# Two local-attention layers of a fused block: the softmax division moved from the probabilities to the mixed values, through a DRAM copy of the reciprocals, with new instruction orders

## The chip, the cores and the metric

The kernel runs on one core of one Trainium2 chip. A core has TensorE (PE; its weight loads are listed apart as PEld), VectorE (DVE), ScalarE (ACT), GpSimd (POOL) and SyncE (SP), which here only issues DMAs. The metric is device time in microseconds (us) of one execution; lower is better. Each engine works through its own list of instructions in order, and waits on semaphores where it needs another engine's result.

## The reference

32 sequences of 256 rows by 128 columns in float32 pass through four residual blocks: full attention with 16 heads and a feed-forward layer; causal attention with rotary positions; and two layers, each of local attention and a gated feed-forward. Only the local attention is touched. For each of its 8 heads of 64 columns:

```python
sim  = einsum('bhwid,bhwjd->bhwij', bq, bk)     # l2-normed, rotary q and k; window of 64 plus the one before
sim  = where(mask, -finfo.max, sim)
attn = softmax(sim, axis=-1)
out  = einsum('bhwij,bhwjd->bhwid', attn, bv)   # heads joined, then x = x + out @ wo
```

## The kernel before

The work of one sequence is cut into six streams, written as digits in the orders: 0 is the first attention with its feed-forward (ATTN0), 1 the causal attention (ATTN1), 2 and 3 the two local attentions (LOCAL0, LOCAL1), 4 and 5 the feed-forward layers behind them (FEED0, FEED1). A stream is a list of units ("qkv2", "scores2", "turn_p", ...), and a unit has a share of work on some of the engines. Different sequences are in work at one time, one stream's behind the other's.

Each engine's order is written out by hand as strings of digits: FIRST fills the pipeline, TURNS is repeated ROUNDS times, and LAST drains it. One repetition (a round) takes one unit list of each stream, so one sequence's worth of work. FIRST and LAST together hold 954 units of each engine's list, a round 159, so they hold six sequences' worth and the 26 rounds the other 26. The eight PSUM banks are handed out by strings of digits too. STEADY_FILLERS and END_FILLERS name units ahead of which PE runs matmuls without use (L1031), which keep it busy where it would wait; 488 are issued in all, 11 of them in each round.

The local attention's softmax: "scores2" fills two banks with queries 0 to 127 and then four with queries 128 to 255 (L1206, L1212); DVE takes negated maxima (L980); ACT takes the exponent with a running sum (L792) into P0, which lies in rawP, and P1, both in SBUF; "norm2", in two halves of four heads, makes reciprocals of the sums on DVE (L987) and multiplies P0 and P1 in place (L990); "turn_p" transposes one head's probabilities on PE (L1224 to L1226), and waits at heads 0 and 4 for the half of norm2; ACT copies them out (L797); "mix2" multiplies with the values (L1239), four heads a bank, and DVE copies the bank to o2T, which lies in rawB (L917); "project2" follows (L1247), and DVE adds the residual into YB (L941).

SP serves three kinds of unit: "residual" loads the next sequence (L583), "shift_rows" moves rows of YB to feed_h (L589, L590), "finish" stores an output (L595). Before each it waits for its own condition, in order.

Of the kernel before, what the change touches and what calls it, by code (L numbers as in the profile page):

```python
# [9 lines left out]
P = 128  # L10
# [17 lines left out]
def shape_constants():  # L28
# [29 lines left out]
    def table(c, s):  # L58
# [15 lines left out]
ROUNDS = 26  # L74
# [4 lines left out]
        "0000000000000000000000000000000000000000000000111100000010000111010011000000100000011100001001100111"  # L79
        "1000101111002222111112221001022202222220111100112222222220000100202111000002222220000102202221101102"  # L80
        "1121000110110022111112222210144442220222221111010140442002222224132220000333003332023330003333300222"
        "2221110000210202220211011200110333333333130113113002222333333111110013333312222223011110311444402222"
        "2444002222222242255551353335000050020250001233"
    ),
    "scalar": (
        "0000000000000000000000000000000000000000001110000000010010000111100000000000000011111100001111111000"
        "0000011110022111111222221001002222222211112222222220000000200220000111111002222220000122222111111000"
        "0000111102220021111112222214444122200111122222004442222222322200000003330033322000033300333332222221"
        "1111100001222221111000000110333333333301111332220022211111133333300133333122222211110044444222224442"
        "2222222225555333333000000055500220000111123345"  # L90
    ),
    "vector": (
        "0000000000000000000000000000000000010001000000000110000100000000001111101100000010000000001111001111"
        "0111111111000012222221120012220000222222200001111122220111222220000020220000000022222011110110222220"
        "2111111111114414222222110000001222222002222211111100222244440000401333333222223000002012330003333333"
        "3222222000000022222001111211433331111114333331113113140000222222003111003333333333222232222222511111"
        "0012254444522004001033333315555222220000002250"
    ),
    "gpsimd": (
        "0000000000000000000000000000000000101111000000000000000000000000000000001111111111101111111111111112"  # L100
        "2222112221222222222222000000000000000000000000000000001111111111111111111111111442222222222222222222"
        "2222221112122222220444444222222200000000000000000000000000000003333333333303333333331111111111111111"
        "1111111114412222222222222222222222222211221222222222422205554444400000000000000000000000000555553333"
        "3333333333333333333333000000001111111122222222"
    ),
    "sync": (
        "0000000000000000000000000000000000000000000000000000000000000000000000000000000000000000000004000000"
        "0000000000000000000000000004444444450000000000000000000000000000000000000000001111111111111111111111"
        "1111111111111111111111111111111111111111111111111111111111111111111111111111112222222222222222222222"
        "2222222222222222222222222222222222222222222222222222222222222222222222222222222222222233333333333333"  # L110
        "3333333333333333333333333333333344444445555555"
# [4 lines left out]
        "3333002222200001210102222101201123333311003033333331330113113002222111113333330031133303444422232222"  # L116
        "22221111301401244022222220422132300003305555505550250001233"
    ),
    "scalar": (
        "3003332222200001112222211113333311300000003333333330111133222002333333221111110013333314444222222111"  # L120
        "12222200424422222222233300000003555553300555220000111123345"
    ),
    "vector": (
        "3003333333333222222000000111102222201102433331111114333331113110000313224222200333331100133333222232"
        "22222255111110012244442200540050122222333333555510000020520"
    ),
    "gpsimd": (
        "3333333333311133311111111111111442222222222222222251112122444444222222222222550000000000000000000000"
        "00000000333333333333333333333333330555555001111111122222222"
    ),  # L130
    "sync": (
        "4550000000000000000000000000000000001111111111111111111111111111122222222222222222222222222222222222"
        "22222333333333333333333333333333333333333333344444445555555"
# [4 lines left out]
        "3100222223330000120333333102222011201121133333333300101103113020211111220333330311333332220222222221"  # L138
        "3111031144440444222222222200413555553333330000555002201133315222222122222112333332113333333311313113"
        "1132222111112223333331333333444412224311114412222224222222222315555531332555233311153331222222112222"  # L140
        "2112333332113333333333111311322224444222333333333332223434422222243322222222333335555533325552253333"
        "3322222222222333333333233233333333333344443444433333333335555555533333333333333333533333333333335555"
        "55555115"
    ),
    "scalar": (
        "3100222223330000133333312222211111133333333300000000111133222002221111113333300313331332222222222211"
        "1100444444422222222223335555533333300000005550022111113331222222122222113333311333333331133111133222"
        "2221111113333332223333314444412221111444222222222222222333555555333555221111133313331222222112222211"
        "3333311333333333311113322222244444333333222333332224443332222222222222333555555233323335552233333322"
        "2222222223333333333333333333333444444443333333333335555555553333333333333333333333333333555555555011"  # L150
        "12233455"
    ),
    "vector": (
        "3002333333333300000222220011112222202033111133111133333111300001144132222220031110023333333333222222"
        "2222435511111100222244454000045103333155553332222220000225333333333322222222223324111133111111411333"
        "3311131131322222223333341133333132222222222554444111112222545113333222223355155225333323333333222221"
        "1112222211233334111111433333111314332222222333332233333222222223444445522225533333335555222222333333"
        "3333522332222233222223333332333333344433333344444555333333353333333333555533333333333533333333333355"
        "55555555"
    ),  # L160
    "gpsimd": (
        "3353333333333111113311111111111112222222222222222221112244222222222244444422550000000000000000000000"
        "0000000033333333333333333333333335555553333333331111111111133311531133111111111114422222222222222222"
        "2222222222211222444444122222222255333333333333333333333335335555533333353311111111111311333113331111"
        "1111442222222222222222222222222222444444222222222222553333333333333333333333333555555333333333333333"
        "4444444455533333333333333333333333333333333313333333555555555555555522222222222222222222333333333333"
        "33333333"
    ),
    "sync": (
        "5455555555544444444555555555444444445444444445555555555555555550000000000000000000000005555555500000"  # L170
        "0111111111111111111111111111111111111111111111111111111111111111111111111112222222222222222222222222"
        "2222222222222222222222222222222222222222222222222222222222222222222222222222222222222222222222222222"
        "2222222333333333333333333333333333333333333333333333333333333333333333333333333333333333333333333333"
        "3333333333333333333333333333333333333333333333333333333333333333333333333333333333333333333333333333"
        "34444444"
    ),
}
FIRST_BANKS = (
    "6704365530407614536573225450135701574201526701547040270216460734252673765021624735015647135023047562"
    "1732072413462505231403062564073240156752135461327050327650411705347357012455265347156207561454071536"  # L180
    "1720450635426537210265410653207615260357132065426312504617325041643013675236103752405167265263762451"
    "6475304052174571054603125034761520163241034257504136273506325470231542106437126034741526307134251674"
    "1067453123056102736045372067513245703642707351203476103642753167524375046310120571324507316254741530"
    "27161235647131067574014356204"
)
# [157 lines left out]
def fused_block(nc, x, wqkv0, w1_0, b1_0, w2_0, b2_0, wqkv1, wo1, wqkv2, q_scale, k_scale, wo2,  # L343
# [7 lines left out]
    with ExitStack() as ctx:  # L351
# [651 lines left out]
        def _(pe):  # L1003
# [13 lines left out]
            def unit(u):  # L1017
# [198 lines left out]
                elif u.kind == "turn_p":  # L1216
# [5 lines left out]
                    for sem, count in newest(free(u)):  # L1222
                        pe.wait_ge(sem, count)
# [77 lines left out]
```

## Time and profile before

| | us |
|---|---|
| median of 3 runs | 2964.49 (2964.08 to 2968.03) |
| the profiled execution's own time | 2968.08 |
| its span, first to last instruction | 2966.4 |
| PE busy | 2714.0 (91%) |
| DVE busy | 2337.2 (79%) |
| ACT busy | 2126.4 (72%) |
| POOL busy | 1606.6 (54%) |

Busy time is a union of an engine's instructions; matmuls overlap one another, so the mean of one times the count is more than the busy time. The share is over the whole span, with its filling and draining.

### The profile page before, as it was taken

Reading aid. Unit: us, or ns where it says so; the run is one execution under the profiler, and the core shown is the slowest. Engines: PE = TensorE matmul, PEld = TensorE weight load, DVE = VectorE, ACT = ScalarE, POOL = GpSimd, SP = SyncE. Lnnn points to the kernel's source line nnn. Section 1 sums busy time; section 2 is a strip of 40 time slices with the busy share of each in tenths; the row PEclk is TensorE's granted clock in tenths of the full one; section 3 lists DMA queues with packets and bytes.
Section 4 is the critical chain, followed back from the end, with each engine's and each line's share of the span. In section 5 each row is a group of like instructions: output and inputs, shape, how many; then the busy total and the mean of one; then the engine's idle time right before and its main releaser. Section 6 shows DMA issues by size and latency. Waiting matters only on the chain.

```text
span 2966.4 us, 69962 instructions
## 1 busy us (share of the span) xinstructions
PE 2714.0 (91%) x24680; PEld 1949.3 (66%) x24680; DVE 2337.2 (79%) x5888; ACT 2126.4 (72%) x5956; POOL 1606.6 (54%) x1747
## 2 busy tenths in 40 slices
PE   5778999999999999999999999999999999999887
PEld 3445666666666676666667666666766666676665
DVE  3467778888888888888888888888888888887764
ACT  2356687777778777877877777787777778777663
POOL 1035455565555556555655655565565556556653
PEclk8889999999999999999999999999999999999999
DMA  2000000000000000000000000000000000000000
GB/s 80 3 3 4 5 4 7 5 6 7 7 7 4 7 5 6 7 7 7 5 6 5 6 7 7 7 5 6 5 7 6 7 7 5 6 7 5 5 3 8
DMA packets 41990, 22.72 MB, mean 8 GB/s; under 512 B 21130, under 2 KB 40884, under 8 KB 41652
## 3 DMA queue, kind: packets, MB, share of 16 engines
q1 hardware_dynamic: 41652, 18.24, 2.2%
q8 instruction: 209, 3.42, 0.5%
q14 instruction: 129, 1.06, 0.1%
HBM read 9.86 MB, written 4.19 MB: 5 GB/s over the span
## 4 chain that ended last, share of the span: by engine, by line
PE 53%; ACT 25%; DVE 16%; issue 3%; POOL 2%; DMA 0%; SPq 0%; DVEq 0%; POOLq 0%; ACTq 0%
PE bank L1175 8%; DVE negmax L900 7%; PE bank L1075 6%; ACT P L792 5%; ACT probs L760 5%; PE bank L1247 4%; PE bank L1186 4%; PE bank L1140 3%; PE bank L1255 3%; ACT rawP L792 3%; PE bank L1239 3%; PE bank L1031 3%; PE bank L1212 3%; PE bank L1096 2%; PE bank L1206 2%
## 5 line engine op out<-in xcount | busy, mean ns | idle before, releaser
L760 ACT ACTIVATE probs<-bank 128x512 f32<-128x512 f32 (+1 forms) x1024 | 478.1, 568 | 206.2 <-PE bank L1119 205.4
L900 DVE TENSOR_REDUCE negmax<-bank 128x2 f32<-128x512 f32 (+1 forms) x896 | 555.1, 683 | 54.4 <-PE bank L1096 40.5
L1175 PE MATMUL bank<-wqkv_sb,hS 128*128 128x512 f32 x768 | 399.8, 623 | 23.2 <-ACT rawA L797 12.4
L692 POOL TENSOR_TENSOR rn<-ss_kept,minus_half 128x16 f32<-128x16 f32 x128 | 372.7, 2912 | 64.8 <-DVE ss_kept L960 64.8
L637 POOL TENSOR_TENSOR veps<-moments,eps_tile 128x2 f32<-128x2 f32 x192 | 38.9, 203 | 641.9 <-DVE moments L852 640.8
L659 POOL TENSOR_SCALAR_AFFINE_SELECT probs<-probs 128x256 f32<-128x256 f32 x512 | 200.2, 413 | 234.8 <-ACT probs L760 234.5
L1140 PE MATMUL bank<-probs,V 128*16 128x256 f32 (+1 forms) x4096 | 246.7, 359 | 25.1 <-POOL probs L659 18.4
L680 POOL TENSOR_TENSOR rawA<-rawA,rope_sb 128x512 f32<-128x512 f32 x128 | 186.3, 1456 | 90.4 <-ACT rawA L779 90.3
L980 DVE TENSOR_REDUCE negmax<-bank 128x2 f32<-128x384 f32 (+1 forms) x384 | 207.1, 595 | 35.0 <-PE bank L1212 34.8
L680 POOL TENSOR_TENSOR rawB<-rawB,rope_sb 128x512 f32<-128x512 f32 x128 | 177.7, 1388 | 85.5 <-ACT rawB L779 85.3
L792 ACT ACTIVATE P<-bank,negmax 128x192 f32<-128x192 f32 x512 | 208.4, 453 | 5.2 <-DVE negmax L980 3.4
L914 DVE COPY rawC<-bank 128x256 f32<-128x256 f32 x256 | 105.7, 414 | 130.1 <-PE bank L1140 129.9
L1175 PEld LDWEIGHTS bank<-wqkv_sb,hS 128*128 128x128 f32 x768 | 125.4, 192 | 106.8 <-issue 78.3
L1255 PE MATMUL bank<-feed_hT,w_sb 128*128 128x256 f32 (+1 forms) x768 | 189.0, 390 | 3.6 <-ACT feed_hT L721 1.3
L1140 PEld LDWEIGHTS bank<-probs,V 128*16 128x16 f32 x4096 | 96.1, 96 | 146.2 <-issue 67.7
L751 ACT ACTIVATE qT<-bank 128x512 fp32r<-128x512 f32 x256 | 153.8, 667 | 45.7 <-PE bank L1075 45.5
L946 DVE TENSOR_REDUCE ss<-P 128x8 f32<-128x512 f32 x256 | 173.1, 676 | 16.4 <-ACT P L776 12.6
L792 ACT ACTIVATE rawP<-bank,negmax 128x128 f32<-128x128 f32 x512 | 180.2, 377 | 6.3 <-DVE negmax L980 5.7
L1031 PE MATMUL bank<-ident_r 128*128 128x512 f32 x488 | 162.0, 449 | 23.1 <-ACT P L792 8.7
L687 POOL TENSOR_TENSOR rawA<-rawA,rawQ 128x512 f32<-128x512 f32 x128 | 163.7, 1279 | 33.6 <-DVE probs L868 33.6
L751 ACT ACTIVATE kT<-bank 128x512 fp32r<-128x512 f32 (+1 forms) x256 | 145.7, 646 | 45.0 <-PE bank L1186 43.6
L687 POOL TENSOR_TENSOR rawB<-rawB,rawP 128x512 f32<-128x512 f32 x128 | 175.5, 1371 | 0.0
(140 smaller groups left out, 7293.7 us busy)
## 6 DMA issues: line engine op xcount, KB each, us to landing
xin<-x SPq DMA_DIRECT2D x32, 128.0 KB, 2.1
out<-xout SPq DMA_DIRECT2D x32, 128.0 KB, 1.8
feed_h<-YB SPq DMA_DIRECT2D x64, 63.5 KB
wqkv_sb<-wqkv SPq DMA_DIRECT2D x1, 1536.0 KB
feed_h<-YB SPq DMA_DIRECT2D x64, 0.2 KB
rawQ<-c_masks SPq DMA_DIRECT2D x1, 832.0 KB
w_sb<-w SPq DMA_DIRECT2D x1, 682.0 KB
w_sb<-w SPq DMA_DIRECT2D x2, 256.0 KB, 2.9
```

The costliest lines, as they stand in the source:

```text
L680: nc.gpsimd.tensor_tensor(raw, raw, tab, ALU.mult).then_inc(sig("cos_part", u), 1)
L687: nc.gpsimd.tensor_tensor((q2, k2)[m][:, l, t, :], (q2, k2)[m][:, l, t, :], sines[m][:, l, t, :], ALU.add)\
L692: nc.gpsimd.tensor_tensor(rn[:, l, t].rearrange("p m h -> p (m h)"), ss_kept[:, l, t].rearrange("p m h -> p (m h)"), minus_half[:], ALU.po ...
L751: nc.scalar.activation(dst[:, 2 * u.part:2 * u.part + 2, :].rearrange("p g q -> p (g q)"), tile(u)[:], ACT.Copy).then_inc(has_emptied(u), 1)
L760: nc.scalar.activation(dst, src, ACT.Exp, scale=SCALE0 if k == ATTN0 else SCALE1)\
L792: last = nc.scalar.activation(dst, src, ACT.Exp, bias=negmax[:, k, t, hd:hd + 1], accum_out=expsum[:, l, t, hd:hd + 1])
L900: nc.vector.reduce_max(negmax[:, k, t, head:head + 4 * many - 3:4], tile(u, e)[:, :].rearrange("p (h k) -> p h k", h=many), AX.X, negate=T ...
L980: nc.vector.reduce_max(dst, src, AX.X, negate=True).then_inc(sig("max_done", u), 1)
L1031: mm(tile(u, spare)[:].rearrange("p (a k) -> p a k", a=4), ident_r[:], ident_r[:].unsqueeze(1).broadcast_to([P, 4, P]), start=True, stop=T ...
L1140: last = mm(tile(u)[32 * n:32 * n + 16, q0:SEQ], V[:, k, t, 4 * g + n, :], part, start=t == 0, stop=t == 1)
L1175: mm(tile(u)[:], hS[:, l, t * P:(t + 1) * P], wqkv2_sb[:, l, m * INNER:(m + 1) * INNER], start=True, stop=True).then_inc(has_filled(u), 1)
L1255: last = mm(tile(u)[0:n, half * SEQ:(half + 1) * SEQ], w1_2_sb[:, l, half * HID + at:half * HID + at + n], hT[k], start=True, stop=True)
```

## The change

"norm2" goes. A unit "spread2" of each local layer takes its place: DVE makes all reciprocals in one instruction of 128x16; PE transposes them, two instructions of 128x8, into rows of heads; ACT copies 8x256 to SBUF (recip_T); SP writes these 8 KB to DRAM (recip_kept), waits until they have landed, and issues two DMAs which each read one 4 KB line back to 64 partitions, 256 KB each, into recip_rows, which is the place of kT2. "turn_p" waits for the exponents alone. DVE's copy of the mixed values becomes a multiplication with recip_rows, and the first of the two waits for the DMAs.

```diff
-    units += [Unit("norm2", half, rec_done=1, p_ready=1) for half in range(2)]
+    units += [Unit("spread2", bank=1, rec_done=1, rows_out=16, rows_spread=2 * 16)]
...
+        recip_rows = kT2
+        recip_T = sb("recip_T", [HEADS, 2, SEQ])
+        recip_kept = nc.dram_tensor("recip_kept", (2, 2, PAIRS * SEQ), f32, kind="Internal").ap()
...
+                elif u.kind == "spread2":     # SP
+                    for sem, count in newest(taken(u)):
+                        sp.wait_ge(sem, count)
+                    sp.dma_start(recip_kept[l].rearrange("e (c q) -> (e c) q", c=PAIRS), recip_T[:, l, :])\
+                        .then_inc(sig("rows_out", u), 16)
+                    sp.wait_ge(sig("rows_out", u), so_far("rows_out", u) + 16)
+                    for e in range(2):
+                        sp.dma_start(recip_rows[HD * e:HD * e + HD, l, :, :].rearrange("p c q -> p (c q)"),
+                                     recip_kept[l, e].partition_broadcast(HD)).then_inc(sig("rows_spread", u), 16)
...
+                elif u.kind == "spread2":     # ACT
+                    nc.scalar.activation(recip_T[:, l, :], tile(u)[0:HEADS, 0:SEQ], ACT.Copy).then_inc(has_emptied(u), 1)
...
                 elif u.kind == "mix2":        # DVE
+                    if u.part == 0:
+                        dve.wait_ge(sig("rows_spread", u), so_far("rows_spread", u))
-                    nc.vector.tensor_copy(o2T[:, l, 2 * u.part:2 * u.part + 2, :].rearrange("p c q -> p (c q)"), tile(u)[:])\
+                    nc.vector.tensor_tensor(o2T[:, l, own, :].rearrange("p c q -> p (c q)"), tile(u)[:],
+                                            recip_rows[:, l, own, :].rearrange("p c q -> p (c q)"), ALU.mult)\
...
-                elif u.kind == "norm2":       # DVE
-                    nc.vector.reciprocal(recip[:, k, :, own], expsum[:, l, :, own]).then_inc(sig("rec_done", u), 1)
-                    for t, part, n in ((0, P0[:, l, own], P), (1, P1[:, l, own, WINDOW:SEQ], SEQ - WINDOW)):
-                        last = nc.vector.tensor_tensor(part, part, recip[:, k, t, own].unsqueeze(2).broadcast_to([P, 4, n]), ALU.mult)
+                elif u.kind == "spread2":     # DVE
+                    nc.vector.reciprocal(recip[:, k, :, 0:HEADS].rearrange("p t (e c) -> p t c e", e=2),
+                                         expsum[:, l, :, :].rearrange("p t (c e) -> p t c e", e=2)).then_inc(sig("rec_done", u), 1)
...
+                elif u.kind == "spread2":     # PE
+                    pe.wait_ge(sig("rec_done", u), so_far("rec_done", u) + 1)
+                    for t in range(TT):
+                        last = turn(tile(u)[0:HEADS, t * P:(t + 1) * P], recip[:, k, t, 0:HEADS], ident)
```

All orders and bank strings are new. There are 27 rounds of 157 units, and FIRST and LAST hold 785 units, five sequences' worth. Where the old strings take long runs of one stream, the new ones change streams almost at every digit:

```diff
 TURNS "tensor"
-        "3333002222200001210102222101201123333311003033333331330113113002222111113333330031133303444422232222"
+        "2223410120244400224152235054435030030033202333005103255030233232121000012022221103350331123011023333"
...
-STEADY_FILLERS = {(ATTN0, "scores", 1): (3, 0), (ATTN0, "maxes", 1): (3, 1), (ATTN1, "scores", 0): (3, 0), (LOCAL0, "qkv2", 0): (2, 0)}
+STEADY_FILLERS = {(LOCAL1, "mix2", 1): (4, 0), (LOCAL1, "spread2", 0): (3, 0), (LOCAL0, "scores2", 1): (3, 0)}
```

A new round has 10 fillers and the whole kernel 452. In a new round the units that PE's list has between the two parts of "scores2", and from there to "spread2", are these. LOCAL0: "down0", three fillers, the second part, a "qkv2" of LOCAL1, "down2", a "turn", a "qkv2" of LOCAL1, "spread2". LOCAL1: a "turn" of ATTN1, "project1", the second part, a "mix" and a "scores" of ATTN0, "shift", three fillers, "spread2". DVE's list has between "spread2" and the first "mix2" of LOCAL0: two "qkv2" and two "scale2" of LOCAL1, "down2", two "qkv" of ATTN0; of LOCAL1: an "apply" of ATTN1, two "qkv2" and "norms2" of LOCAL0, two "mix" of ATTN0, two "qkv" of ATTN1. ACT's list has just ahead of the first "scores2" two "up0" for LOCAL0, and a "scores" of ATTN0 and a "turn" for LOCAL1. PE's list has between "spread2" and the first "mix2" four "turn_p" and seven to nine units of other streams.

## Rows read from the trace of the kernel before

**Rows 1.** Busy time by stretch: PE, PEld, DVE, ACT, POOL, clock, DMA share, GB/s.

```profile
0.00:200.00 200.00, 133.99 (x1016) 87.41 (x1016) 92.56 (x260) 72.18 (x158) 44.69 (x70) 0.84 0.10 32
...
1000.00:1500.00 500.00, 476.57 (x4476) 343.37 (x4476) 418.26 (x1058) 379.71 (x1059) 287.39 (x316) 1.00 0.02 6
...
1507.46:1593.81 86.35, 82.25 (x768) 59.34 (x767) 72.42 (x184) 66.10 (x188) 50.19 (x55) 1.00 0.02 6
```

**Rows 2.** Chain of work that ended last, 1500 to 1700 us: start, us, what.

```profile
1507.46 1.10 DVE rawP L990
...
1587.63 1.28 ACT L792
1588.92 2.90 ACT rawP L792 x16
...
1593.81 1.10 DVE rawP L990
1594.90 1.94 DVE P L990
...
1603.64 0.89 PE bank L1031 x3
...
1604.98 0.89 PE bank L1031 x3
...
1680.11 1.11 DVE rawP L990
```

**Rows 3.** Groups by line and shape, whole span: count, busy us, mean ns, idle before.

```profile
L990 DVE TENSOR_TENSOR P<-P,recip 128x768 f32<-128x768 f32 x128 | 150.3, 1174 | 0.0
L990 DVE TENSOR_TENSOR rawP<-rawP,recip 128x512 f32<-128x512 f32 x128 | 100.5, 785 | 4.4
L987 DVE RECIPROCAL recip<-expsum 128x8 f32<-128x8 f32 x128 | 24.8, 194 | 15.5 <-ACT P L792 15.3
L923 DVE RECIPROCAL recip<-bank 128x16 f32<-128x16 f32 x128 | 32.1, 251 | 49.7 <-PE bank L1147 49.7
L917 DVE COPY rawB<-bank 128x512 f32<-128x512 f32 x128 | 86.9, 680 | 15.5 <-PE bank L1239 15.4
L946 DVE TENSOR_REDUCE ss<-P 128x8 f32<-128x512 f32 x256 | 173.1, 676 | 16.4 <-ACT P L776 12.6
L951 DVE TENSOR_TENSOR rawQ<-bank,rope_sb 128x256 f32<-128x256 f32 x128 | 52.7, 411 | 0.0
L969 DVE TENSOR_TENSOR rawB<-rawB,rn 128x512 f32<-128x512 f32 x128 | 100.9, 788 | 2.0 <-POOL rawB L687 2.0
L724 ACT ACTIVATE probs<-bank 128x256 f32<-128x256 f32 x128 | 55.2, 431 | 128.7 <-PE bank L1052 128.6
L1168 PE MATMUL bank<-w_sb,rawC 128*128 128x128 f32 x512 | 64.6, 280 | 1.1 <-issue 1.0
```

**Rows 4.** DMA issues, whole span: count, KB each, median us to landing.

```profile
xin<-x SPq DMA_DIRECT2D x32, 128.0 KB, 2.1
out<-xout SPq DMA_DIRECT2D x32, 128.0 KB, 1.8
...
w_sb<-w SPq DMA_DIRECT2D x2, 256.0 KB, 2.9
```

**Rows 5.** The same chain, 2780 to 2967 us.

```profile
2945.62 0.56 SPq L589
2946.23 5.37 DMA feed_h<-YB
```

**Rows 6.** SP's queue: waits in all, times, longest us.

```profile
SPq L588 <- DVE YB L941: 1578.6, 64, 44.2
```

**Rows 7.** The chain again, 1500 to 1700 us: single units of PE and ACT.

```profile
1539.56 0.71 PE bank L1153 x4
1540.27 0.90 PE bank L1206 x8
1541.17 0.66 PE bank L1212 x7
1541.85 0.57 DVE negmax L980
1542.44 3.33 ACT P L792 x16
...
1546.44 2.07 ACT probs L760 x4
...
1565.29 0.51 PE bank L1119 x8
...
1568.62 0.99 PE bank L1140 x16
...
1575.22 1.34 PE bank L1263 x12
...
1578.36 0.37 PE bank L1052 x2
...
1581.57 0.86 PE bank L1175 x2
...
1585.09 1.46 ACT rawC L766 x4
```

More of the change, by code:

```diff
@@ L156 @@
[L156 to L159, printed above, removed]
+        "1331222222225111105244405222540001053532232213351025102030223313233353333112212323322123331323111131"
+        "1214314131422342312211321333233332223252211222121152444223545152222513233332523123523231323313333231"
@@ L168 @@
+        "3432333332533343423333322434333343342333254532333333332333335533335355333525335533235332232333555353"
+        "325335333"
     ),
     "sync": (
[L170 to L173, printed above, removed]
@@ L176 @@
+        "33555555555"
     ),
@@ L196 @@
+    "432337435162741562156236036476504610"
 )
-STEADY_FILLERS = {(ATTN0, "scores", 1): (3, 0), (ATTN0, "maxes", 1): (3, 1), (ATTN1, "scores", 0): (3, 0), (LOCAL0, "qkv2", 0): (2, 0)}
+STEADY_FILLERS = {(LOCAL1, "mix2", 1): (4, 0), (LOCAL1, "spread2", 0): (3, 0), (LOCAL0, "scores2", 1): (3, 0)}
 END_FILLERS = {
-    (0, ATTN0): {("turn_q", 0): 5, ("mix", 0): 7, ("mix", 1): 7, ("mix", 2): 7, ("mix", 3): 7, ("turn", 0): 8},
-    (1, ATTN0): {("turn_q", 0): 5, ("mix", 0): 7, ("mix", 1): 3, ("mix", 2): 7, ("turn", 0): 8},
-    (31, LOCAL1): {("qkv2", 2): 9, ("turn_p", 0): 10},
-    (31, FEED1): {("turn", 0): 28},
+    (0, ATTN0): {("maxes", 1): 6, ("maxes", 2): 4, ("maxes", 3): 7, ("mix", 0): 7, ("mix", 2): 4},
+    (1, ATTN0): {("maxes", 1): 6, ("maxes", 3): 6, ("mix", 0): 7},
+    (0, LOCAL0): {("shift", 0): 5, ("turn_q2", 0): 6},
+    (1, LOCAL0): {("shift", 0): 5},
+    (2, ATTN1): {("maxes", 0): 6},
+    (30, LOCAL0): {("shift", 0): 6},
+    (31, ATTN1): {("maxes", 1): 4},
+    (31, LOCAL0): {("scores2", 1): 7},
+    (30, LOCAL1): {("spread2", 0): 11},
+    (30, FEED1): {("turn", 0): 8},
+    (31, LOCAL1): {("turn_q2", 0): 6},
+    (31, FEED1): {("turn", 0): 27, ("down2", 0): 5},
@@ L1216, in unit @@
                 elif u.kind == "turn_p":
+                    needs = [free(u)]
                     if u.part % 4 == 0:
-                        made = earlier(u, "norm2", u.part // 4)
-                        pe.wait_ge(sig("p_ready", made), so_far("p_ready", made) + 1)
+                        first, second = (taken(earlier(u, "scores2", n)) for n in range(2))
+                        needs += [first, second[0:2]] if u.part == 0 else [second[2:4]]
                     hd, bank = u.part, tile(u)
-                    for sem, count in newest(free(u)):
+                    for sem, count in newest(*needs):
                         pe.wait_ge(sem, count)
```

140 lines of the change are left out of this document (65 added, 75 removed).

## The prediction

> **What bounds the kernel now.** I read the busy time by stretch first [rows 1]. In the middle PE is busy 476.6 of 500 us, DVE 418.3, ACT 379.7, at a granted clock of 1.00; at the start PE has 134.0 of 200 at 0.84. So there are two parts, a steady one and two ends. Then the chain [rows 2]: the same multiplication of rawP (L990) stands at 1507.46 and at 1680.11, two rounds later, so a round is 86.33 us. In one round [rows 1] PE is busy 82.25 us and idle 4.1, and DVE is busy 72.4.
>
> 26 rounds take 2244.6 us, which leaves 721.8 us of the span of 2966.4 for the ends, with six sequences' worth of units. Six rounds would be 518.0; the ends therefore cost 203.8 us beyond their work.
>
> The chain says what holds the round. It passes from engine to engine: ACT's table load and exponents (1.28, 2.90, 1.62), then 1.10 + 1.94 us of L990 on DVE, later PE, with six fillers in it (0.89 + 0.89) [rows 2]. The reader is to see that the removed multiplication stands in a place where the work behind it waits: 3.04 us in each round.
>
> **What goes.** L990 is 150.3 + 100.5 us in all [rows 3], 7.84 us a sequence on DVE. The four reciprocals of 128x8 (194 ns) become two of 128x16, nearest the 251 ns of L923 [rows 3]: 0.27 us less. On DVE's list that is 8.1 us of 72.4. Only what is on the chain counts for the end: 3.04 us a round. The rest of L990 (4.8 us a round) is in the chain nowhere, and I count it as nothing; if the chain came to pass there, the round could shrink on, and then PE's own work stands in the way, which is the first rival.
>
> **What comes in its place.** The mixed values' multiplication reads PSUM and SBUF, 128x512. Its bounds are the copy that it replaces, 680 ns (L917), and a multiplication of that shape with both inputs in SBUF, 788 ns (L969) [rows 3]; four times a sequence 0 to 0.4 us, and I take 0, since with PSUM as one input it is nearer the copy.
>
> PE gets four transposes a sequence. A "turn" of two has 0.37 us [rows 7], so at most 0.74 us and, with only 8 columns to load, not under 0.2; I take 0.44. It loses one filler of 0.30 [rows 2]. Net 0.1.
>
> ACT gets two copies of 8x256. The nearest is 128x256, 431 ns (L724) [rows 3]. ACT's stretch of the chain holds one of them: 0.43 us. Nothing or both would be 0 or 0.86.
>
> The sum for a round: 86.33 - 3.04 + 0.1 + 0.43 = 83.8 us.
>
> **The trip through DRAM.** After the last exponent: reciprocal 0.25, transposes 0.4, copy 0.43, write, read. No row shows a write of 8 KB or two reads of 256 KB. For the write the nearest are the store of an output, 1.8 us, and the load of a sequence, 2.1 [rows 4]; the farthest is feed_h, whose issue and landing take 0.56 + 5.37 us [rows 5]. For the reads the nearest is a 256 KB load, 2.9 us [rows 4], for both together if they overlap and 5.8 if not. I take 2.1 + 3.5, because the sizes are those of the first rows, so 6.7 us in all. With 0.2 for the transposes, 1.8 and 2.9 it is 5.6, with 0.74, 5.93 and 5.8 it is 13.1.
>
> The Trainium skill (DMA: Bandwidth & Descriptors, Anatomy of one DMA) speaks against such a trip: each DMA has a fixed cost of about 2.0 us, mostly the receipt of the write, heaviest to HBM, and bytes come on top at 436 GB/s. As an estimate from that page the write and the two reads overlapped would be 5.2 us in place of 5.6. The trace's 1.8 to 2.9 us for 128 to 256 KB agrees; no run here shows the small write. Neither changes the round.
>
> What hides it: PE has four turn_p and seven to nine other units before "mix2", and DVE has two qkv2 (2 x (0.68 + 0.41 + 0.41) = 3.0 us) and, in LOCAL0, two scale2 (1.6) before it multiplies [rows 3]. So DVE, held at the head of its list, may wait 6.7 - 4.6 and 6.7 - 3.0, at most 5.8 us a round, and at the far bound 18.6. Behind it wait ATTN0's maxima in LOCAL0 and LOCAL1's next qkv2, and PE for their banks. DVE is then busy 64.4 of 83.8 us: idle 19.4. I take the wait as covered by that. SP's own list is held through write and issue, some 3 us twice a round; behind it stand shift_rows and the loads, and SP now waits up to 44.2 us for them [rows 6], so this is nothing.
>
> **The ends.** FIRST and LAST go from 954 to 785 units. The 203.8 us may shrink with the units, to 167.7, or stay, if they are one sequence's latency; nothing shows which, and I take the middle, 186.
>
> Span: 32 x 83.8 + 186 = 2868. The profiled execution's own time was 1.7 us over its span, and the median 3.6 below that own time, so 1.9 less: **2866 us**.
>
> **Rivals.**
>
> *Deeper* (chance 0.17). Without the stop at norm2, the six fillers in the chain fall out of it too: 83.8 - 1.8 = 82.0, and the ends go with the units: 32 x 82.0 + 168 = 2792, reported 2790. For it: the fillers stand where PE waited for DVE. Against it: this is under PE's 82.25 busy us of today. But a busy PE here overlaps its matmuls: single units run at 0.86 us for two of 512 columns [rows 7]. The Trainium skill (Perfetto Trace Analysis, Identifying the Most-Contended Engine) says the same: matmul busy share is no measure of how near PE is to its peak, weight loads are. The trace has those at 59.3 of 86.35 us [rows 1], which by that rule leaves room below 82.
>
> *Elsewhere* (0.17). A path beside L990, of nearly its length, takes over, for DVE's freed time is spread and PE and ACT have as much to do as before. The round stays 86.3: with ends of 186 a reported 2947, with 204 no change, 2965. For it: PE is idle in many short gaps, not one. I give two thirds to the first, since fewer units are in the ends.
>
> *Slower* (0.18). In PE's list "spread2" stands soon after "scores2", and waits for the last exponent and the reciprocal, with everything of PE's behind it. From the end of the first "scores2", ACT's side is [rows 7, 2] maximum 0.57, load 1.28, exponents 2.90 + 3.33, reciprocal 0.25: 8.3 us in LOCAL0, and 7.05 without a load in LOCAL1. PE's side in LOCAL0: down0 2.0 (64.6 us over 32, L1168 [rows 3]), fillers 0.9, second part 0.90 + 0.66, qkv2 0.86, down2 1.34, turn 0.37, qkv2 0.86: 7.9. In LOCAL1: turn 0.37, project1 0.71, second part 1.56, mix 0.99, scores 0.51, shift 0.37, fillers 0.9: 5.4. PE waits 0.4 + 1.65 = 2.05 us a round, if ACT is at once free; in its list two up0 (1.46) and an ATTN0 scores (2.07) stand just ahead, so up to 5.6. The forecast takes these waits to fall into the 4.1 us a round that PE is idle today. If that idle time stays beside them, all of it lengthens the round, and it decides from 3.3 us: (2972 - 186) / 32 = 87.1, against 83.8. Half-way from there to the top, 4.4: 32 x 88.2 + 186 = 3008, reported 3006. Against it: the second part needs PE at once, but the first part's exponents are half done by then.
>
> **How the numbers follow.** The forecast has 0.48. A measurement of this kernel can tell about 0.2%, 6 us. Faster: 0.48 + 0.17 + 0.11 = 0.76; same 0.06; slower 0.18. The range goes from 2775, half a us a round (16 us) under the deeper case, to 2970, the no-change end of the third rival; the slower case and a little of the deeper one are left out. The forecast's own range, with 0.1 to 0.8 us each way on ACT's and PE's terms and 167.7 to 203.8 for the ends, is 2830 to 2900.
>
> **What would show it.** Right: L990 gone, the distance between repeats of one line near 83.8 us, DVE busy near 64 of it, ACT near 67, PE idle under 4 us, and the chain passing from the exponents into turn_p. The multiplication near 0.7 us. The DMA's landing before DVE comes to mix2, so that its list of waits has little for recip_rows. Wrong: a wait of PE for the reciprocal at spread2 of over 3 us a round (slower); the chain through SP's DMAs and DVE's multiplication (the trip is not hidden, which a landing over 10 us would do); a round of 86 us with DVE idle (elsewhere); a granted clock under 1.00 in the middle, since gaps would then cost PE's speed as well.

## The result and the profile after

The changed kernel takes 3013.31 us (median of 4 runs, 3012.73 to 3014.28) against 2964.47 (2964.08 to 2968.03) for the kernel before: a ratio of 1.0162, 95% interval 1.0145 to 1.0180. It is slower, by 49 us or 1.6%: clear of the noise, though less than 2%. Forecast were 2866 us and a range from 2775 to 2970.

The first view is busy time by stretch, columns as in [rows 1]: 500 us of the middle, then three neighbouring rounds of the changed kernel. A round is taken here from one last addition of an output on POOL to the next.

```profile
1000.00:1500.00 500.00, 470.59 (x4433) 339.87 (x4435) 380.20 (x981) 381.54 (x1072) 275.45 (x309) 0.99 0.07 19
1527.62:1615.67 88.05, 83.09 (x772) 60.03 (x771) 67.00 (x173) 66.68 (x189) 48.52 (x55) 0.98 0.07 18
1615.67:1703.75 88.08, 83.16 (x773) 60.42 (x772) 66.95 (x173) 66.66 (x189) 48.47 (x55) 0.98 0.07 18
1703.75:1790.40 86.65, 81.71 (x772) 59.47 (x771) 66.67 (x173) 66.67 (x189) 48.48 (x55) 1.00 0.07 18
```

Against the round in [rows 1], DVE's busy time fell from 72.4 to 67.0 us, and ACT has 66.7 as forecast; still no round is under 86.6. There are two kinds of round: 16 of 24 take 88.0 to 88.1 us at a clock of 0.98, every third about 86.65 at 1.00. This pattern runs through the whole steady part. Read in windows of 0.1 us, 24 rounds from the first have a mean of 87.59 us; those of before have 86.39.

So the 46.2 us between the spans (3012.6 and 2966.4) divide as follows. 26 rounds take 2277.1 us where before's would take 26 x 86.39 = 2246.1: 31.0. Of these, 26 x (87.59 - 86.65) = 24.4 come from the rounds with the lower clock, the other 7 from 86.65 against 86.39. What lies around these 26 rounds, six sequences' worth of work in both kernels, grew from 720.3 to 735.5: 15.2.

The chain of work that ended last, in one stretch of such a round (start, us, what):

```profile
1579.66 1.79 PE bank L1265 x16
1581.67 1.13 PE bank L1100 x13
1583.51 1.58 ACT probs L768 x3
1586.26 1.84 PE bank L1149 x16
1588.10 3.42 PE bank L1273 x12
...
1675.57 4.05 PE bank L1273 x12
```

L990 is gone from the chain [rows 2]. In its place PE's own matmuls are the chain: by engine, PE holds 67% of the span in the page's chain and DVE 17%, where before it was 53% and 16%, with 25% on ACT. And the same twelve matmuls of "up2" (L1273) that take 2.79 us in the round ahead of these (at 1500.52, a short one) take 3.42 and 4.05 here. Why is told by windows of 1 us, same columns; the first five from the round that starts at 1527.62, the last four from the one that starts at 1703.75:

```profile
1583.00:1584.00 1.00, 0.48 (x16) 0.27 (x12) 1.00 (x5) 0.49 (x1) 0.22 (x1) 1.00 0.02 0
1584.00:1585.00 1.00, 0.00 (x0) 0.00 (x0) 1.00 (x3) 1.00 (x4) 1.00 (x1) 1.00 0.06 12
1586.00:1587.00 1.00, 1.00 (x16) 0.32 (x12) 0.87 (x3) 0.88 (x1) 1.00 (x2) 0.50 0.08 18
1588.00:1589.00 1.00, 1.00 (x6) 0.84 (x3) 1.00 (x4) 0.00 (x0) 1.00 (x1) 0.50 0.00 0
1590.00:1591.00 1.00, 1.00 (x7) 0.76 (x6) 0.82 (x2) 0.61 (x2) 0.92 (x2) 1.00 0.00 0
...
1760.00:1761.00 1.00, 0.00 (x0) 0.00 (x0) 1.00 (x3) 1.00 (x3) 1.00 (x1) 1.00 0.04 10
1761.00:1762.00 1.00, 0.69 (x21) 0.72 (x24) 1.00 (x3) 0.98 (x3) 1.00 (x1) 1.00 0.08 18
1762.00:1763.00 1.00, 1.00 (x28) 0.45 (x20) 0.93 (x3) 1.00 (x1) 1.00 (x2) 1.00 0.08 17
1764.00:1765.00 1.00, 1.00 (x6) 0.88 (x5) 1.00 (x3) 0.47 (x1) 1.00 (x2) 1.00 0.01 1
```

PE stops at the same place in both rounds. In the first the granted clock then falls to 0.50, the lower of its two levels (1.2 GHz), from 1586 to beyond 1589; in the other it stays at 1.00. The clock behind the stop costs 1.4 us (88.05 and 86.65); what the stop costs without it is left to run 3. PE's timeline names the place (start, us, what, idle before it):

```profile
1582.63 0.56 PE L1105 MATMUL bank<-kT,qT 32*128 32x128 f32 x16
1583.03 0.45 PE L1128 MATMUL bank<-qT,kT 32*128 32x256 f32 x8
1585.18 0.51 PE L1105 MATMUL bank<-kT,qT 32*128 32x256 f32 x8 [1.71 <-ACT probs L768]
```

L1105 is ATTN1's "maxes", L1128 ATTN0's "scores". The new order of PE has ATTN1's first "maxes" (banks 2, 6, 1, 4), ATTN0's last "scores" (0, 7, 5, 3) and ATTN1's second "maxes" (2, 5, 7, 6) right behind one another: twelve uses of eight banks, so PE waits for ACT's exponents (L768) to give a bank back. Before, an "up2" and a "mix" of one bank each stood between the two "maxes" (0347, then 5 and 6, then 0423), and neither kernel has fillers there. The old order has twelve uses in a row at another place (ATTN0's first "maxes" 4017, ATTN1's first "scores" 2546, ATTN0's second "maxes" 2310), and there three fillers stand ahead of the second unit and three ahead of the third.

The change's own parts, by groups (line, shapes, count, busy us, mean ns, idle before) and DMA issues:

```profile
L931 DVE TENSOR_TENSOR rawB<-bank,kT 128x512 f32<-128x512 f32 x128 | 87.7, 686 | 68.4 <-PE bank L1257 48.6 <-DMA kT<-recip_kept 19.7
L1243 PE MATMUL bank<-ident_r,recip 128*8 128x128 f32 x128 | 24.7, 275 | 16.2 <-DVE recip L999 16.2
L809 ACT ACTIVATE recip_T<-bank 8x256 f32<-8x256 f32 x64 | 23.0, 359 | 2.4 <-PE bank L1243 2.4
L999 DVE RECIPROCAL recip<-expsum 128x16 f32<-128x16 f32 x64 | 16.3, 254 | 59.6 <-ACT P L800 58.1
...
kT<-recip_kept SPq DMA_DIRECT2D x128, 256.0 KB, 3.8
...
out<-xout SPq DMA_DIRECT2D x32, 128.0 KB, 3.6
```

The multiplication takes 686 ns (the copy had 680 [rows 3]), the reciprocal 254, ACT's copy 359, the two reads 3.8 us. DVE idles for the DMA in 7 of its 128 multiplications, 19.7 us in all, and the list of waits has none of these in five rounds of the middle: the trip is hidden.

DVE's busy time fell by 5.4 us a round and not by the 8.1 that were to go. The largest part of the rest is a multiplication that the change does not touch and that takes longer in the new orders; first before, then after:

```profile
L969 DVE TENSOR_TENSOR rawA<-rawA,rn 128x512 f32<-128x512 f32 x128 | 93.1, 728 | 10.2 <-POOL rawA L687 10.1
```
```profile
L984 DVE TENSOR_TENSOR rawA<-rawA,rn 128x512 f32<-128x512 f32 x128 | 133.0, 1039 | 9.0 <-POOL rawA L695 6.6 <-issue 0.3
```

Without the DMAs of the reciprocals (run 4) it still takes 1037 ns, so it is not they; what it is stays open.

### The profile page after: what moved, and what is told of

It reads as the page before. It is cut to its first block, busy times and chain, and to the rows that moved or that the text cites. A ratio compares the mean times of both kernels' runs of the same rounds, so it can differ in the third digit from the quotient of the medians.

```text
span 3012.6 us, 70452 instructions
## 1 busy us (share of the span) xinstructions
PE 2732.9 (91%) x24772; PEld 1966.2 (65%) x24772; DVE 2154.7 (72%) x5568; ACT 2145.9 (71%) x6020; POOL 1561.6 (52%) x1747
## 4 chain that ended last, share of the span: by engine, by line
PE 67%; DVE 17%; ACT 8%; issue 4%; POOL 1%; DMA 1%; DVEq 0%; SPq 0%; POOLq 0%; ACTq 0%
DVE negmax L911 8%; PE bank L1184 8%; PE bank L1273 6%; PE bank L1084 6%; PE bank L1149 5%; PE bank L1257 4%; PE bank L1195 4%; PE bank L1265 4%; ACT P L800 4%; PE bank L1067 3%; DVE negmax L995 3%; PE bank L1221 3%; PE bank L1105 2%; PE bank L1215 2%; ACT probs L768 2%
## 5 line engine op out<-in xcount | busy, mean ns | idle before, releaser
L768 ACT ACTIVATE probs<-bank 128x512 f32<-128x512 f32 (+1 forms) x1024 | 472.5, 548 | 204.9 <-PE bank L1128 204.2
L645 POOL TENSOR_TENSOR veps<-moments,eps_tile 128x2 f32<-128x2 f32 x192 | 49.9, 260 | 609.8 <-DVE moments L863 609.0
L1149 PE MATMUL bank<-probs,V 128*16 128x256 f32 (+1 forms) x4096 | 262.3, 376 | 10.7 <-ACT probs L768 5.5
L1273 PE MATMUL bank<-feed_hT,w_sb 128*128 128x256 f32 (+1 forms) x768 | 206.7, 416 | 6.4 <-DVE up2T L1005 3.4
L688 POOL TENSOR_TENSOR rawB<-rawB,rope_sb 128x512 f32<-128x512 f32 x128 | 165.3, 1292 | 70.7 <-ACT rawB L787 70.7
L759 ACT ACTIVATE qT<-bank 128x512 fp32r<-128x512 f32 x256 | 140.0, 597 | 85.7 <-PE bank L1084 85.6
L1105 PE MATMUL bank<-kT,qT 32*128 32x256 f32 (+1 forms) x2048 | 117.8, 313 | 87.4 <-ACT probs L768 57.6
L1273 PEld LDWEIGHTS bank<-feed_hT,w_sb 128*128 128x128 f32 (+1 forms) x768 | 145.7, 198 | 71.7 <-issue 25.4
L695 POOL TENSOR_TENSOR rawB<-rawB,rawP 128x512 f32<-128x512 f32 x128 | 162.8, 1272 | 54.4 <-DVE probs L879 54.4
L813 ACT ACTIVATE up2T<-bank,b_sb 128x256 f32<-128x256 f32 (+1 forms) x192 | 90.6, 473 | 130.8 <-PE bank L1273 128.0
L1105 PEld LDWEIGHTS bank<-kT,qT 32*128 32x128 f32 x2048 | 82.4, 187 | 141.6 <-DVE negmax L911 57.4
```

The costliest lines, as they stand in the source:

```text
L688: nc.gpsimd.tensor_tensor(raw, raw, tab, ALU.mult).then_inc(sig("cos_part", u), 1)
L768: nc.scalar.activation(dst, src, ACT.Exp, scale=SCALE0 if k == ATTN0 else SCALE1)\
L1105: last = mm(tile(u, e)[:, i * keys:(i + 1) * keys], qT[rows, k, first + i, t * P:(t + 1) * P], kT[rows, k, first + i, 0:keys], start=not w ...
L1149: last = mm(tile(u)[32 * n:32 * n + 16, q0:SEQ], V[:, k, t, 4 * g + n, :], part, start=t == 0, stop=t == 1)
L1273: last = mm(tile(u)[0:n, half * SEQ:(half + 1) * SEQ], w1_2_sb[:, l, half * HID + at:half * HID + at + n], hT[k], start=True, stop=True)
```

## The experiments

Two theories stood after this profile. **Clock** (Theory A in the expectations): the stop at ATTN1's second "maxes" and the clock behind it are the loss. **Change's own**: the reciprocal's way is, by PE's wait at "spread2" (Theory B) or by DVE's wait for the DMAs (Theory C). Beside them stood the forecast's own question: what is L990 worth in the chain?

| run | us | ratio to before, 95% | clock | mean round |
|---|---|---|---|---|
| before | 2964.47 | | 0.982 | 86.39 |
| after | 3013.31 | 1.0145 to 1.0180 | 0.968 | 87.59 |
| 1 old orders, new arithmetic | 3173.01 | 1.0670 to 1.0710 | 0.953 | 93.12 |
| 2 new orders, old arithmetic | 3190.20 | 1.0716 to 1.0790 | 0.939 | 93.53 |
| 3 after, two fillers at "maxes" | 2986.52 | 1.0052 to 1.0086 | 0.980 | 86.66 |
| 4 after without the trip | 3009.46 | 1.0129 to 1.0163 | 0.970 | 87.47 |
| 5 after without the division | 3024.98 | 1.0180 to 1.0211 | 0.968 | 88.14 |
| 6 before without the division | 2957.57 | 0.9952 to 0.9978 | 0.983 | 85.90 |
| 7 run 1 without the trip | 2988.35 | 1.0059 to 1.0089 | 0.981 | 86.78 |
| 9 run 3, seven fillers fewer | 2981.87 | 1.0039 to 1.0069 | 0.983 | 86.67 |
| 10 after, one "up2" moved | 2990.33 | 1.0065 to 1.0095 | 0.980 | 86.82 |
| 11 run 10, seven fillers fewer | 2985.62 | 1.0047 to 1.0077 | 0.979 | 86.83 |
| 12 before, six fillers fewer | 2983.94 | 1.0039 to 1.0072 | 0.971 | 86.97 |
| 13 run 6, six fillers fewer | 2958.55 | 0.9964 to 0.9986 | 0.978 | 86.24 |

Clock is the mean granted clock of the profiled execution; the mean round is over 24 rounds, by the outputs' additions. The intervals are those of the ratio to runs of the kernel before on the same chip (2966.73 us beside runs 10 to 13). Runs 4 to 7 and 13 leave out the division or part of its way, so they compute something else. The profiled execution of run 6 is the fastest of its five (2950.13 us; the others take 2957.4 to 2957.6). There is no run 8.

**Runs 1 and 2: each half alone.**

```diff
 # 1: on before; orders, banks and fillers as they were, but for spread2's bank, its place in ACT's list, and SP's list
-    units += [Unit("norm2", half, rec_done=1, p_ready=1) for half in range(2)]
+    units += [Unit("recip2", rec_done=1), Unit("spread2", bank=1, rows_out=16, rows_spread=2 * 16)]
 # 2: on after; one norm2 (both halves) where spread2 stood
-    units += [Unit("spread2", bank=1, rec_done=1, rows_out=16, rows_spread=2 * 16)]
+    units += [Unit("norm2", rec_done=2, p_ready=2)]
```

> The old orders, banks and fillers, with the new arithmetic put into them: the reciprocals at the place of the first norm2, transposes, copy and DMAs at that of the second. Theory A (the loss lies in the new orders: a stop of PE with no fillers in it, after which the granted clock falls in most rounds): the arithmetic by itself costs nothing or helps, 2900 to 2965 us. Theory B (PE's wait for the reciprocal at spread2 is the loss, some 2.5 us a round): this one waits as well, 2990 to 3040 us. Theory C (DVE held by the DMAs at mix2): in these orders DVE comes to mix2 sooner after the reciprocal, over 3040 us.

> The new orders, with norm2 (both halves) at the place of spread2, no transposes, copies or DMAs of reciprocals. Theory A: the stop and the falling clock stay, and DVE has its 8 us a round back, 3010 to 3080 us. Theory B: PE has no spread2 to wait at, but turn_p waits for the multiplications, so between 2940 and 3010 us. Theory C: 2940 us or less.

Both are some 7% slower, rounds of 93 us. Run 1 lies in the range of Theory C; Theory A had the arithmetic cost nothing there, and missed. Run 2 lies above all the ranges. In run 1 the trip has come into the chain; its largest wait of DVE over the span, and two lines of its chain:

```profile
DVE rawB L985 <- DMA kT<-recip_kept: 215.8, 59, 9.1
...
1508.89 1.28 DMA recip_kept<-recip_T
1510.79 4.79 DMA kT<-recip_kept
```

In run 2 PE stops at "turn_p" for a bank that DVE empties late: its list has both halves of norm2, 5.9 us, ahead of that:

```profile
1515.58 0.33 PE L1220 MATMUL bank<-ident_r,rawP 128*128 128x128 f32 x1 [3.57 <-DVE rawQ L948]
```

So the new orders hide the trip, where the old ones with spread2 in this place do not, and the old arithmetic does not fit the new orders. Whether another place in the old orders would hide it was not tried. Both runs also lose by the clock: in 24 rounds it falls to 0.50 in 34 stretches of run 1 and in 51 of run 2. The rounds at a clock of 1.00 take 90.1 to 90.3 us in run 1 and 89.9 in run 2.

**Run 3: fillers at the stop.**

```diff
-... (LOCAL0, "scores2", 1): (3, 0)}
+... (LOCAL0, "scores2", 1): (3, 0), (ATTN1, "maxes", 1): (2, 0)}
```

> The changed kernel with two more fillers in each round, ahead of ATTN1's second maxes, in the bank that comes free first, where PE stops for 1.7 us and the clock falls behind it. Theory A: the clock stays at 1.00, 1.0 to 1.4 us a round are won, 2970 to 2985 us. Theory B and C: two fillers more and nothing won, 3013 to 3030 us.

Two matmuls without use in each round save 27 us. The clock is 1.00 all through the middle, and every round takes 86.6 to 87.0 us: the long rounds are gone, and no short one got shorter. That is the clock theory, and its size (24.4 us in the steady part). The stop without the falling clock cost nothing: filled, the round is as long as the short rounds that have it. The time is 1.5 us over the range of Theory A.

**Runs 4 and 5: the change's own costs, in the new orders.**

```diff
 # 4: no SP part; mix2 multiplies by a constant tile in SBUF
-    recip_rows[:, l, own, :].rearrange("p c q -> p (c q)"), ALU.mult)
+    wqkv2_sb[:, l, 0:512], ALU.mult)
 # 5: spread2 empty on all engines; mix2 copied; its three fillers ahead of turn_p
-                elif u.kind == "spread2":   # PE, ACT, DVE, SP
```

> The changed kernel without the DMAs of the reciprocals: mix2 multiplies by a tile of weights and waits for no DMA, so the division is left out; reciprocals, transposes, copies and fillers stay. DVE's list of waits in the changed kernel shows next to nothing for recip_rows, so the trip is hidden in these orders and this is within 0.5% of the changed kernel, 3000 to 3020 us. If the trip is on the path, 2960 us or less.

> The changed kernel with no division at all: no reciprocals, transposes, copies, DMAs and multiplications of them (mix2 is copied out as before); the softmax's division is left out. Its three fillers of spread2 stand before turn_p. Theory A: turn_p waits for the same exponents, the stop at maxes stays, 2985 to 3010 us. Theory B: some 2.5 us a round are won, 2920 to 2945 us. Theory C: 2940 us or less.

Without the trip 4 us are saved, as expected. Without reciprocals, transposes, copies, trip and multiplication the kernel is no faster (run 5 lies above all three ranges) and has the long rounds more often, 20 of 24. Run 5 is not a clean removal: "spread2" and its fillers had covered PE's wait ahead of LOCAL0's first "qkv2", and now PE stops there too:

```profile
1570.55 1.12 PE L1159 MATMUL bank<-wqkv_sb,hS 128*128 128x512 f32 x2 [1.32 <-ACT hS L724]
```

But the rounds in which the clock holds have only the stops themselves and no slow matmuls behind them: they take 86.65 us after, 86.57 in run 4 and 86.86 in run 5. Taking out the change's own arithmetic wins nothing back there either.

**Runs 6 and 7: the same parts in the old orders.**

```diff
 # 6: norm2 empty; turn_p waits for the exponents only
-    units += [Unit("norm2", half, rec_done=1, p_ready=1) for half in range(2)]
+    units += [Unit("pause2", half) for half in range(2)]
 # 7: run 1 without the SP part; mix2 multiplies by a constant tile
```

> The kernel before, orders, banks and fillers unchanged, with norm2 left out and nothing in its place: the softmax's division is left out, turn_p waits for the exponents alone. It is the most that any replacement of norm2 can give in these orders. If the step of 3.04 us a round on the chain was right, 2964 falls by some 95 us, to 2860 to 2880. If the freed time of DVE is worth little, because PE's list and its banks hold the round, 2930 to 2966.

> The old orders with the new arithmetic, without its DMAs: reciprocals, transposes and copies are made, mix2 multiplies by a tile of weights in place of the spread reciprocals and waits for no DMA, so the division is left out. If the DMAs' landing is what makes the old orders with the new arithmetic 207 us slower than before, this is within 40 us of the kernel without the division, under 3000 us. If spread2 on PE and ACT (its bank, its wait) is, it stays over 3100 us.

Run 6 lies in the range expected if the freed time of DVE is worth little, run 7 in that of a costly landing. Run 6 is the most that any way of dropping norm2 could give in these orders: 85.90 us a round in place of 86.39 in the profiled execution, 9 us in all by the medians. Run 7 adds the new arithmetic without its trip: 86.78, so 0.88 us a round. Run 1's other 6.3 us a round come with the trip: some 3.4 of them are there in its rounds at a clock of 1.00, the rest comes in the rounds with the lower clock.

Why so little? The timelines of before and of run 6 show what stands behind the last exponents of LOCAL0 (start, us, what, idle before it). L724 is ACT's first instruction behind them, L946 DVE's next work, and L1075, in run 6 L1064, PE's transposes of ATTN0's queries and keys. First before, then run 6:

```profile
1594.86 0.47 ACT L724 ACTIVATE probs<-bank 128x256 f32<-128x256 f32 x1
1594.83 2.02 DVE L990 TENSOR_TENSOR P<-P,recip 128x768 f32<-128x768 f32 x1
1596.77 0.67 DVE L946 TENSOR_REDUCE ss<-P 128x8 f32<-128x512 f32 x1
1598.98 1.09 PE L1075 MATMUL bank<-ident_r,QB 128*128 128x128 f32 x8 [0.55 <-DVE KB L893]
```
```profile
1585.75 0.47 ACT L724 ACTIVATE probs<-bank 128x256 f32<-128x256 f32 x1
1586.74 0.69 DVE L946 TENSOR_REDUCE ss<-P 128x8 f32<-128x512 f32 x1 [2.67 <-ACT P L776]
1589.35 1.09 PE L1064 MATMUL bank<-ident_r,QB 128*128 128x128 f32 x8 [0.21 <-DVE KB L893]
```

Without L990 DVE is free earlier, but its next work needs squares (P, L776) that ACT makes only behind the exponents, so DVE stands idle for 2.67 us. From L724 to PE's transposes it is 4.12 us before and 3.60 in run 6, and much the same in every other steady round: 0.52 less, which is about the 0.49 of the round. The path beside L990 runs over ACT's list, which has the squares and then the copies of ATTN0's "qkv" that the transposes wait for.

**Run 9: fewer fillers on run 3.**

```diff
-... {(LOCAL1, "mix2", 1): (4, 0), (LOCAL1, "spread2", 0): (3, 0), (LOCAL0, "scores2", 1): (3, 0)}
+... {(LOCAL1, "spread2", 0): (3, 0), (ATTN1, "maxes", 1): (2, 0)}
```

> The changed kernel with the two fillers ahead of ATTN1's second maxes, and without the seven ahead of scores2 (LOCAL0, second part) and mix2 (LOCAL1, second part), which stand in the chain of waits with 0.70 and 0.93 us a round. If they only cost PE time, the clock stays at 1.00 and the 2986 us of the kernel with all twelve fall to 2930 to 2960. If they hold the clock there, it falls in those places, and the time is 2990 to 3040 us.

Seven fillers of some 0.3 us fewer in each round change the round by nothing (86.66 and 86.67): they stand where PE would wait; the 5 us between the times lie outside these rounds. The time lies between the two ranges. Where four of the fillers stood, ahead of "mix2", PE now stops for 1.0 us in each of the 24 rounds, and the clock stays at 1.00:

```profile
1644.83 0.77 PE L1257 MATMUL bank<-rawA,V 128*64 128x192 f32 x8 [1.04 <-ACT rawQ L805]
```

It is the fastest variant of the changed kernel, and still 0.4 to 0.7% slower than before.

**Runs 10 and 11: useful work at the stop.** One "up2" of FEED0, with its bank, goes ahead of ATTN1's second "maxes".

```diff
-        "22234101202444...        "3526140753257610374...
+        "22234104120244...        "3526140753025761374...
```

> The changed kernel with one unit moved in PE's list: FEED0's first up2, which stood behind ATTN0's last mix, now stands between ATTN0's last scores and ATTN1's second maxes, where PE stops 1.7 us and the granted clock falls to 0.50; nothing is added. If the stop and the clock behind it are the loss: the clock stays at 1.00 in the steady part, the round goes from 88.04 to 86.3 to 87.0 us, as with the two fillers or a little better, time 2960 to 2990. If PE must wait that long for ACT's exponents whatever stands there, since up2 takes a bank of the same scores: the round stays at 87.6 to 88.2, time 3000 to 3015.

> The same with the seven fillers a round at LOCAL1's second mix2 and LOCAL0's second scores2 left out (three a round remain, ahead of LOCAL1's spread2). If these fillers only take PE's time: up to 7 x 0.3 = 2.1 us a round less, time 2900 to 2950. If they stand where PE would wait anyway, as the run with moved fillers showed (5 us in all): 2955 to 2985. If one of the places is a stop that they cover, the granted clock falls there and the time is over 2995.

PE's timeline in run 10, around the place of the stop:

```profile
1575.46 0.46 PE L1128 MATMUL bank<-qT,kT 32*128 32x256 f32 x8
1576.69 1.10 PE L1273 MATMUL bank<-feed_hT,w_sb 128*128 128x256 f32 x4 [0.77 <-ACT probs L768]
1577.72 0.51 PE L1105 MATMUL bank<-kT,qT 32*128 32x256 f32 x8
```

The stop of 1.71 us is 0.77, the granted clock stays at 1.00, the round is 86.82, with nothing added to PE's work: the clock theory again, by another hand. Both times lie at the upper edge of the range expected for that. Run 11 shows once more that the other seven fillers are free in the steady part.

**Runs 12 and 13: the six fillers in the chain of before [rows 2].**

```diff
-STEADY_FILLERS = {(ATTN0, "scores", 1): (3, 0), (ATTN0, "maxes", 1): (3, 1), (ATTN1, "scores", 0): (3, 0), (LOCAL0, "qkv2", 0): (2, 0)}
+STEADY_FILLERS = {(ATTN1, "scores", 0): (3, 0), (LOCAL0, "qkv2", 0): (2, 0)}
```

> The kernel before with the six fillers a round that stand in its chain (ATTN0's second scores and second maxes) left out; five a round remain. The prediction's deeper case had them fall out of the round without a price, 1.8 us: time 2905 to 2915. If they cover a wait for DVE that stays: 2955 to 2970. If the stop that they cover brings the granted clock down, as at the second maxes of the changed kernel: clock under 1.00 in the steady part, time 2985 to 3030.

> The same six fillers left out of the kernel before without any division (2957.6 us, round 85.9). The computation lacks the division by the sums. If PE's own work holds the round once norm2 is gone: 6 x 0.3 = 1.8 us a round less, time 2895 to 2910. If the maxima on DVE and exponents on ACT hold it where the fillers stand: 2945 to 2965. If the stop brings the clock down: over 2975.

Two neighbouring rounds of run 12, then windows of 1 us in the second, and the stop in PE's timeline:

```profile
1519.46:1605.74 86.28, 80.47 (x762) 58.41 (x761) 72.37 (x184) 66.09 (x188) 50.13 (x55) 1.00 0.02 6
1605.74:1693.35 87.61, 82.09 (x762) 59.06 (x761) 72.54 (x184) 66.20 (x188) 50.12 (x55) 0.98 0.02 6
...
1642.00:1643.00 1.00, 0.34 (x8) 0.33 (x8) 1.00 (x6) 1.00 (x6) 0.00 (x0) 1.00 0.00 0
1643.00:1644.00 1.00, 0.58 (x10) 0.20 (x2) 0.96 (x5) 1.00 (x7) 0.57 (x2) 1.00 0.00 0
1646.00:1647.00 1.00, 1.00 (x2) 0.34 (x1) 1.00 (x2) 1.00 (x3) 0.00 (x0) 0.50 0.00 0
...
1642.66 0.51 PE L1119 MATMUL bank<-qT,kT 32*128 32x256 f32 x8 [0.96 <-ACT P L792]
```

The kernel before shows the same once these fillers go: rounds of 86.3 and 87.6 alternate (11 long ones of 24), the longer ones with a stretch at 0.50 behind a stop of PE, here of 0.96 us ahead of ATTN0's second "scores". Its fillers buy 17 us, and the time is 1 us under the range for a falling clock. And a round in which the clock holds is as long as with them. In run 13 the clock falls in 6 rounds of 24; its time lies in the range expected if maxima and exponents hold the round. A round of run 6, and under it one of run 13:

```profile
1510.96:1596.83 85.87, 82.12 (x768) 59.41 (x769) 65.03 (x171) 66.09 (x187) 48.16 (x55) 1.00 0.02 6
```
```profile
1514.41:1600.29 85.88, 80.36 (x764) 58.43 (x763) 65.03 (x171) 66.00 (x187) 48.05 (x54) 1.00 0.02 6
```

PE is busy 1.76 us less, DVE has 7 us less than before, and the round is 85.9 in both. So it is not PE's or DVE's busy time that holds it.

## Why the prediction was wrong

**The step that failed** is the one read from the chain: "the removed multiplication stands in a place where the work behind it waits: 3.04 us in each round". It does stand there, but its length on the chain is only the most that its removal can give. Run 6 removes all of norm2 and gains 0.49 us a round. Another path, 0.5 us shorter, was waiting beside it: ACT's work behind the exponents, which DVE and PE need next. This is the rival *Elsewhere* (0.17); I argued for it that PE and ACT keep their work, and gave it too little. The chain shows one path, and the idle time of PE and DVE in the round says nothing of the length of the next one.

**The terms of the sum**, in us a round. Dropping norm2: -3.04 forecast, -0.49 measured (run 6; -0.3 by the medians, 9 us over 32). The new arithmetic without its trip: +0.53 forecast, +0.88 measured in the old orders (run 7 less run 6). PE's transposes in it take 0.77 us (24.7 over 32), above the 0.2 to 0.74 allowed for them; how the rest divides is not shown. The trip: 0 forecast; 6.3 in the old orders with the clock that falls (run 1 less run 7), 0.1 in the new ones (after less run 4). From run 7's 86.78 the new orders come, with the trip hidden, to 86.65 where the clock holds, and the clock adds 0.94 in the mean: 87.59. Against 83.8 forecast that is 32 x 3.79 = 121 us of the 145 by which the span was missed (3012.6 and 2868). The other 24 are the ends: 3012.6 - 32 x 87.59 = 209.7, not 186. I had them shrink half-way with their units; they did not shrink. Their clock is 0.87 up to 389 us and 0.95 from 2667, where before had 0.90 up to 429 and 0.97 from 2589; which wait in them costs the rest was not tried.

**What was not in the sum at all** is what new orders can break. I costed the moves around "spread2" alone and let every other place of the round stand as it was. The loss of 24 us comes from a place that the division does not touch, where the new order of PE uses twelve banks in a row and has no filler. That could be read from the new strings: BANKS begins with 35, then 2614, 0753 and 2576, these three units one behind another, and the steady fillers name no "maxes" of ATTN1. The last sentence on what would show it wrong, a clock under 1.00 in the middle, is what happened.

**The rivals.** *Slower* gave 3006 us, and this is 7 us off, but its mechanism is not the cause. Its wait exists: in five rounds (1525 to 1965 us) PE's weight loads wait 9.7 us in all for the reciprocal, 1.9 a round, where 2.05 was worked out. But run 5, which has no "spread2" to wait at, is no faster even where the clock holds, and fillers elsewhere (run 3) win 27 us without touching "spread2". A nearly right time for a wrong reason. *Deeper* had the six fillers fall out of the round for 1.8 us; in the old orders runs 12 and 13 show 0 for it, and a loss where the clock fell. The Trainium skill (Perfetto Trace Analysis, Identifying the Most-Contended Engine), cited for it, sees room below PE's busy time; run 13 agrees so far that PE's 80.4 us are not what holds a round of 85.9, but no run here has a round under 85.8.

**What was right.** ACT's busy time (66.7 us; "near 67" forecast), and DVE's in its direction only (67.0; "near 64"). The multiplication at the copy's price, and nearly the trip: in run 1's chain a write and its reads together take 5.8 to 7.0 us from the start of the write to the end of the reads, where 5.6 were taken from the rows. By the Trainium skill (DMA: Bandwidth & Descriptors, Anatomy of one DMA — SWDGE (gpsimd) path) it was an estimate of 5.2; that section's figures are fitted to DMAs that GpSimd issues, and these are SP's. The rows of loads and stores were the better guide. Also that SP's list has room: it waits 1085.5 us for recip_T over the span.

**What stays open**: what holds the rest of the 85.9 us in the old orders without norm2, and the 86.65 in the new ones. At the place of L990 it is ACT's list; elsewhere the chain of run 6 has maxima on DVE, ACT's exponents and PE's units between them, but no run shortened one of these alone. The ends' 15 us are open too, and why some DVE instructions take longer in the new orders.

## What to carry to other kernels

A step's length on the chain of waits is an upper bound of what taking it off the chain gives; an emptied kernel without the step measures the real value, and here it was 9 us of the 97 that 32 rounds of 3.04 would make. Before costing a step, look at what the engine behind it needs next, and when that is ready. When an order is written anew, go through the whole of it, not only the moved step: count how many banks the engine takes in a row before any can come back, and look for what covers the wait. Emptying a step can uncover a wait that it covered, as in run 5. Fillers are judged by the clock behind them: seven here changed no round, two elsewhere were worth 27 us.

## What the runs showed of the hardware

A stop of PE of 1.7 us is followed in some rounds by some 3 us at a granted clock of 0.50 and in others by none: in the changed kernel in 16 rounds of 24, in run 4 in 15. Which round is hit follows a nearly regular pattern, though each has the same work. The price was 1.3 to 1.4 us a round in three kernels (88.05 and 86.65; 87.6 and 86.3; in run 13 87.3 and 85.9). The length of one stop does not tell by itself. With the stop cut to 0.77 us (run 10), and at stops of 1.0 us ahead of "mix2" (runs 9 and 11), the clock held in all 24 rounds; in run 12 a stop of 0.96 us with two shorter ones close behind it was followed by 0.50 in 11 of 24.

A multiplication of 128x512 on DVE with one input in PSUM took no longer than a copy from there (686 ns; the copy 680 before and 686 in run 5). Those of the same shape with both inputs in SBUF took 728 and 788 before, and 1039 and 869 in the new orders. The store of an output lands in 3.6 us; it had 1.8 [rows 4]. The reads of reciprocals on the same queue do not explain that: without them it takes 5.0 in the new orders (runs 2, 4 and 5), with them 2.6 in the old ones (run 1).
